# A four-block graph network on one core: the first unit's weights load later, mixing groups end with a block, four PSUM places for the first unit's tiles, batch norm by column chunk, the last bias goes into the residual

## The reference

```python
edge_index = jnp.stack([src, dst])
x = _layernorm(x + _L0_gnn_ref(x, ...))   # h = segment_sum(norm * (x @ W.T)[row]) + b; batch norm over nodes; exact gelu; + x
x = _layernorm(x + _L1_gnn_ref(x, ...))   # two layers relu(h @ W_self + mean_of_neighbours(h) @ W_neigh + b)
x = _layernorm(x + _L2_gnn_ref(x, ...))   # two gated relational layers: w = einsum('rb,bio->rio', att, basis), 30 bases, 2 relations, + x @ root + bias
x = _layernorm(x + _L3_gnn_ref(x, ...))   # x = h + segment_sum(h[send]); relu(x @ W1 + b1) @ W2 + b2
```

## Time and profile before

| what | value |
|---|---|
| median of 3 runs | 958.25 us (957.13 to 961.15) |
| profiled execution, its own time | 959.76 us |
| its span | 957.8 us |
| TensorE busy | 899.9 us, 94% |
| DVE busy | 684.1 us, 71% |
| ACT busy | 280.2 us, 29% |
| POOL busy | 85.5 us, 9% |
| mean granted TensorE clock | 0.977 |

### The profile page before, as it was taken

How to read it: one execution, slowest core, us unless ns; L and a number is a source line. 1 busy time by engine, 2 the same in 40 slices (tenths; PEclk the granted TensorE clock), 3 DMA queues, 4 the chain that set the end, 5 groups by cost and what they waited for, 6 DMA issues and landing times.

```text
span 957.8 us, 13083 instructions
## 1 busy us (share of the span) xinstructions
PE 899.9 (94%) x4320; PEld 434.2 (45%) x4320; DVE 684.1 (71%) x1469; ACT 280.2 (29%) x431; POOL 85.5 (9%) x66
## 2 busy tenths in 40 slices
PE   6799999998996999988799799999999999999996
PEld 2354555554554544433344344444444444444442
DVE  6598898854437879798899999999834244442358
ACT  0132345443873313424031211111711131132220
POOL 1000011120111002103021000000600010010000
PEclk9899999999997999999799999999999999999998
DMA  8755565558112495788644675664041014322236
GB/s 285 233 176 155 156 179 163 158 142 186 44 45 67 109 241 167 193 249 160 178 125 128 136 186 157 181 159 116 1 99 34 1 49 115 90 66 44 44 88 195
DMA packets 133371, 126.97 MB, mean 133 GB/s; under 512 B 80417, under 2 KB 80886, under 8 KB 133306
## 3 DMA queue, kind: packets, MB, share of 16 engines
q10 hardware_dynamic: 94784, 57.69, 24.5%
q1 hardware_dynamic: 38522, 68.45, 24.3%
HBM read 95.24 MB, written 12.52 MB: 113 GB/s over the span
## 4 chain that ended last, share of the span: by engine, by line
PE 65%; DVE 19%; DMA 6%; issue 3%; ACT 3%; DVEq 1%; POOL 1%; ACTq 1%; SPq 1%
PE Dp L669 23%; PE Dp L639 22%; PE T L595 9%; PE Dp L551 5%; PE Dp L694 5%; DVE acc L1205 4%; DMA stage<-in_basis 2%; DVE stt L1297 2%; DVE Zraw L1316 1%; DMA wst<-mixd 1%; DVE w L1334 1%; DVE Zraw L1274 1%; DVE S L1282 1%; POOL Zraw L508 1%; DMA Zraw<-in_basis 1%
## 5 line engine op out<-in xcount | busy, mean ns | idle before, releaser
L639 PE MATMUL Dp<-W,hT 128*128 128x512 f16 x816 | 182.9, 383 | 6.6 <-DMA hT<-S 3.2
L669 PE MATMUL Dp<-Zraw,A 128*128 128x512 f16 x800 | 173.0, 379 | 0.0
L1205 DVE SCALAR_TENSOR_TENSOR acc<-stage,att,acc 128x512 f32<-128x512 f32 x232 | 166.6, 788 | 4.0 <-DMA stage<-in_basis 4.0
L669 PE MATMUL Dp<-Zraw,AT 128*128 128x512 f16 x600 | 130.0, 379 | 0.0
L639 PEld LDWEIGHTS Dp<-W,hT 128*128 128x128 f16 x816 | 80.1, 99 | 103.6 <-issue 8.4
L669 PEld LDWEIGHTS Dp<-Zraw,A 128*128 128x128 f16 x800 | 78.3, 98 | 94.4
L1098 DVE TENSOR_SCALAR Zraw<-hT,w 128x640 f16<-128x640 f16 (+1 forms) x240 | 111.1, 463 | 0.1
L669 PEld LDWEIGHTS Dp<-Zraw,AT 128*128 128x128 f16 x600 | 58.7, 98 | 70.8
L1096 DVE TENSOR_SCALAR Zraw<-hT,w 128x128 f16<-128x128 f16 (+1 forms) x240 | 66.7, 278 | 27.0 <-PE Dp L551 18.1
L551 PE MATMUL Dp<-Zraw 128*128 128x320 f16 (+1 forms) x480 | 74.7, 302 | 1.6 <-DVE Zraw L1098 1.0
L922 ACT ACTIVATE Zraw<-Dp,zsc 128x512 f16<-128x512 f32 x50 | 32.2, 684 | 133.7 <-PE Dp L639 131.1
(11 more groups left out here) (169 smaller groups left out, 905.2 us busy)
## 6 DMA issues: line engine op xcount, KB each, us to landing
stage<-in_basis SPq DMA_DIRECT2D x180, 256.0 KB, 2.9
Zraw<-in_basis SPq DMA_DIRECT2D x60, 256.0 KB, 2.9
xres<-w ACTq DMA_DIRECT2D x30, 256.0 KB, 2.3
xr<-xres ACTq DMA_DIRECT2D x30, 256.0 KB, 2.9
wst<-in_Wn ACTq DMA_DIRECT2D x4, 1024.0 KB, 5.7
wst<-in_Ws ACTq DMA_DIRECT2D x4, 1024.0 KB, 5.6
wst<-mixd ACTq DMA_DIRECT2D x4, 1024.0 KB, 5.9
wst<-in_root ACTq DMA_DIRECT2D x3, 1024.0 KB, 5.7
```

Source lines behind the costliest of these rows:

```text
L639: last = nc.tensor.matmul(Dp[:, j, m, :], turned[:, hp, k * P:(k + 1) * P], weights_of(u, m)[:, wp, k, :], start=(n == 0), stop=(n == 3 * ...
L669: last = nc.tensor.matmul(sum_bank(t), a[:, k, ds(t * P, P)], Z[:, r, h, k, :], start=(n == 0), stop=(n == count - 1))
L1205: last = v.scalar_tensor_tensor(part, stage[:, q, :], a, part, ALU.mult, ALU.add)
```

## The change

Six edits:

1. ACT's first step is now the copy-out of mixing group 0; the load of W0 comes behind it. DVE takes W0's maximum behind the maxima of x, before window 10, and no longer before window 4.
2. `GROUP_BLOCKS` gives the seven later mixing groups 6, 6, 6, 6, 5, 5 and 6 windows, so that each group's last product is the last one behind a window.
3. Unit 0's dense tiles go to four PSUM places in turn, two in `Dp` and two in `T`, and tile t waits for DVE's read of tile t-4.
4. `agg_turned` has the column chunk as its outer loop: 20 matmuls fill one bank, then a signal; `block_stats` multiplies that chunk and takes its statistics. There are three parts instead of five, of 512, 512 and 226 columns.
5. Unit 4 adds unit 6's bias to its normalized rows (`w2 = w1 + bias`, a new DVE operation for each tile) and stores that sum to `xres`; the store waits for it (`s_rb`). The bias is loaded behind unit 4's last dense tile, earlier than before.
6. `last_tile` then needs one operation for what were two: `w2 = product * scale + xr`. TensorE's wait for a free PSUM place in unit 6 is now on that operation (`s_v`).

```diff
 MIX_SLOTS = 8
-PARTS = 5
+PARTS = 3
 KEYS = WIN * REL * NT
...
 
+        GROUP_BLOCKS = [6, 6, 6, 6, 5, 5, 6]
+        assert sum(GROUP_BLOCKS) == NWIN and len(GROUP_BLOCKS) == GROUPS - 1
+        SHARES = [(i + 1) * PAIRS // n - i * PAIRS // n for n in GROUP_BLOCKS for i in range(n)]
+
         def mix_share(w):
 
-            rest = PAIRS * (GROUPS - 1)
-            return (w + 1) * rest // NWIN - w * rest // NWIN
+            return SHARES[w]
 
         def groups_done(w):
 
-            rest = PAIRS * (GROUPS - 1)
-            return 1 + (w + 1) * rest // NWIN // PAIRS
+            return 1 + sum(SHARES[:w + 1]) // PAIRS
 
...
             ("agg", 4, 0): [("high", 5, 0)],
-            ("agg", 4, 1): [("bias", 6)],
+            ("dense", 4, 9): [("bias", 6)],
             ("agg", 4, 2): [("load", 6, 0)],
...
 
+        def dense_bank(u, t, m):
+
+            if u == 0:
+                return (Dp[:, 0, 0, :], Dp[:, 1, 0, :], T[:, 0, :], T[:, 1, :])[t % 4]
+            return Dp[:, t % 2, m, :]
+
+        def dense_rows(u, t, m):
+
+            return dense_bank(u, t, m).rearrange("p (a d) -> p a d", a=1)
+
         BACK = {(0, 0): 4, (0, 1): 5, (1, 0): 6, (2, 0): 7, (2, 1): 8, (3, 0): 9}
...
                 low_weights(1, m)
-            pool.wait_ge(s_agg[0], KT)
+            pool.wait_ge(s_agg[0], PARTS * KT)
             pool.wait_ge(s_dout, NT)
...
                     if nz:
-                        wait(pe, s_zlo[u], t - 1)
+                        wait(pe, s_zlo[u], t - 3 if u == 0 else t - 1)
                     if nz == 2:
                         wait(pe, s_zlp[u], t - 1)
-                    if unit["own"] is not None:
+                    if u == NU - 1:
+                        wait(pe, s_v, NT * LN.index(u) + t - 1)
+                    elif unit["own"] is not None:
                         wait(pe, s_own[u], t - 1)
...
                             for k in range(KT):
-                                last = nc.tensor.matmul(Dp[:, j, m, :], turned[:, hp, k * P:(k + 1) * P],
+                                last = nc.tensor.matmul(dense_bank(u, t, m), turned[:, hp, k * P:(k + 1) * P],
                                                         weights_of(u, m)[:, wp, k, :], start=(n == 0), stop=(n == 3 * KT - 1))
...
                     j = b % 2
-                    wait(pe, b_ev, b - 1)
-                    for k in range(NT):
-                        if b == 0:
-                            pe.wait_ge(s_zlo[0], k + 1)
-                        for h in range(2):
-                            for c in range(0, NP, D):
-                                w = min(D, NP - c)
+                    for i in range(PARTS):
+                        c, w = i * D, min(D, NP - i * D)
+                        wait(pe, b_ev, PARTS * (b - 2) + i + 1)
+                        for k in range(NT):
+                            if b == 0 and i == 0:
+                                pe.wait_ge(s_zlo[0], k + 1)
+                            for h in range(2):
                                 last = nc.tensor.matmul(Df[:, j, c:c + w], Z[:, 0, h, k, b * P:(b + 1) * P],
                                                         AT[:, k, c:c + w], start=(k == 0 and h == 0), stop=(k == NT - 1 and h == 1))
-                    last.then_inc(s_agg[0], 1)
+                        last.then_inc(s_agg[0], 1)
 
...
                 if u == 1:
-                    pe.wait_ge(b_ev, KT)
+                    pe.wait_ge(b_ev, PARTS * KT)
                     for t in range(4):
...
 
+            mixed_out(0)
             load_weights(0, 0)
-            mixed_out(0)
             for t in range(NT):
...
                     nc.scalar.activation(S16[:, ds(t, 1), 0:D], w1[:, j:j + 1, :], ACT.Copy, scale=LN_SCALE).then_inc(s_hi[u], 1)
-                    act.dma_start(xres[ds(t * P, P), :], w1[:, j, :]).then_inc(s_xst[u][j], 16)
+                    if u == 4:
+                        act.wait_ge(s_rb, t + 1)
+                    act.dma_start(xres[ds(t * P, P), :], (w2 if u == 4 else w1)[:, j, :]).then_inc(s_xst[u][j], 16)
 
...
                             scale = 2.0 ** -unit["zexp"]
-                        nc.scalar.activation(Z[:, r, 0, ds(t, 1), :], Dp[:, j, r:r + 1, :], ACT.Copy,
+                        nc.scalar.activation(Z[:, r, 0, ds(t, 1), :], dense_rows(u, t, r), ACT.Copy,
                                              scale=scale).then_inc(s_zhi[u], 1)
...
                 link(v.memset(i_in[:, u:u + 1], 1.0 / LN_SCALE))
-            weight_work("counts", 0, 0)
             windows_to(6)
...
             v.tensor_reduce(xin[:, :], xcol[:, :], AX.X, ALU.max).then_inc(s_xin, 1)
+            weight_work("counts", 0, 0)
             windows_to(13)
...
                     dve.wait_ge(s_zhi[u], t * nz + 1)
-                    v.scalar_tensor_tensor(Z[:, 0, 1, ds(t, 1), :], Dp[:, j, 0:1, :], scale,
+                    v.scalar_tensor_tensor(Z[:, 0, 1, ds(t, 1), :], dense_rows(u, t, 0), scale,
                                            Z[:, 0, 0, ds(t, 1), :], ALU.mult, ALU.subtract).then_inc(s_zlo[u], 1)
...
                         normalize(t, j)
+                        if u == 4:
+                            dve.wait_ge(s_bias[6], 16)
+                            dve.wait_ge(s_r, NT * u + t + 1)
+                            v.tensor_tensor(w2[:, j, :], w1[:, j, :], bias_of(6), ALU.add).then_inc(s_rb, 1)
                     else:
...
                     dve.wait_ge(s_d, t + (NT * u + 1))
-                    v.scalar_tensor_tensor(acc[:, 0, j, :], Dp[:, j, 0, :], ownc[:, u:u + 1], bias_of(u),
-                                           ALU.mult, ALU.add).then_inc(s_own[u], 1)
-                    dve.wait_ge(s_own[u], t + 1)
                     tile_moved(dve, s_xl[u], t, j)
                     if isinstance(t, int) and t < 2:
                         dve.wait_ge(s_ready, NT * u + NT - 1 + t)
-                    v.tensor_tensor(w2[:, j, :], acc[:, 0, j, :], xr[:, j, :], ALU.add).then_inc(s_v, 1)
+                    else:
+                        dve.wait_ge(s_r, NT * u + t - 1)
+                    v.scalar_tensor_tensor(w2[:, j, :], Dp[:, j, 0, :], ownc[:, u:u + 1], xr[:, j, :],
+                                           ALU.mult, ALU.add).then_inc(s_v, 1)
                     stats(t, j)
...
 
-                    dve.wait_ge(s_agg[0], b + 1)
-                    v.tensor_tensor(HT[:, b, :], Df[:, b % 2, 0:NP], drow, ALU.mult).then_inc(b_ev, 1)
-                    dve.wait_ge(b_ev, b + 1)
                     for i in range(PARTS):
-                        v.bn_stats(bst[:, b % 2, i * 6:(i + 1) * 6],
-                                   HT[:, b, i * (N // PARTS):(i + 1) * (N // PARTS)]).then_inc(b_st, 1)
+                        c, n = i * D, PARTS * b + i + 1
+                        dve.wait_ge(s_agg[0], n)
+                        v.tensor_tensor(HT[:, b, c:min(c + D, NP)], Df[:, b % 2, c:min(c + D, NP)], drow[:, c:min(c + D, NP)],
+                                        ALU.mult).then_inc(b_ev, 1)
+                        dve.wait_ge(b_ev, n)
+                        v.bn_stats(bst[:, b % 2, i * 6:(i + 1) * 6], HT[:, b, c:min(c + D, N)]).then_inc(b_st, 1)
                     dve.wait_ge(b_st, PARTS * (b + 1))
                     v.bn_aggr(bmv[:, b, :], bst[:, b % 2, :]).then_inc(b_mv, 1)
                     dve.wait_ge(b_mv, b + 1)
```

More of the change, by code:

```diff
@@ L248, in resnorm_gnn_kernel @@
         s_zlp = {u: sem(f"s_zlp{u}") for u in (3, 4)}
-        s_own = {u: sem(f"s_own{u}") for u in (1, 2, 3, 4, 6)}
+        s_own = {u: sem(f"s_own{u}") for u in (1, 2, 3, 4)}
         s_agg = {u: sem(f"s_agg{u}") for u in range(6)}
@@ L259, in resnorm_gnn_kernel @@
         s_gl = sem("s_gl")
+        s_rb = sem("s_rb")
         s_diag = sem("s_diag")
```

## The result

The changed kernel takes 950.65 us, the median of 5 runs (946.62 to 953.21); the kernel before takes 959.58 beside it (957.13 to 961.15, 5 runs). The ratio is 0.9903, with an interval of [0.9882, 0.9924]: 1.0% faster. The profiled execution took 948.84 us, span 946.9 (before 959.76, span 957.8), at a mean granted clock of 0.981 (before 0.977). By the medians the gain is 8.9 us, by the two profiles 10.9.

The account below looks back on a forecast made before the run. The ending chain was two thirds TensorE, a fifth DVE, so only TensorE's idle time or DVE tails could pay. Terms 0 - 2.1 - 3.2 - 2.5 + 0.4 - 3.8 = -11.2 us: profiled 948.6, median 947.0, range 943 to 952.5.

Parts of the forecast that it names:

- W0's load, 0: Start: TensorE begins about 1.5 us sooner, but late W0 may delay group 1's piece; 0, bounds -1.5 and +1.1.
- W0 out of the way: Rival: SP's early start is kept and nearly all of tile 2's wait goes; 944.5 us, chance 0.15.
- W0's maximum, 0: Before window 10: DVE's 2.29 us only changes order; 0, at worst part returns as a wait there.
- Window 10 takes the gain: Rival: DVE's 2.29 us shows whole, W0 collides (+1.1), transposes keep 1.7 of four places; 952.1 us, chance 0.14.
- Groups, -2.1: Windows: four TensorE waits go (-3.0 us), one product is paid later (0.9); bounds -3.0 and -1.0.
- Four places, -3.2: Unit 0's dense tiles: 4.6 us of tile 2's wait and slowness, less 0.5 and 0.9 for transposes; bounds -1.5, -4.6.
- Chunks, -2.5: Unit 0's tail: DVE's 3.2 us after the last matmul becomes 0.75; bounds -1.0 and -2.6 us.
- weight loads come into the open: Rival, slower: 98 ns of all 240 stationary loads exposed in column chunks, 23.5 us; 970.5 us, chance 0.02.
- Unit 4, +0.4: Before unit 5: the store of the sum waits for DVE's new operation, delaying z_out; bounds 0 and 1.0 us.
- unit 6, -3.8: Last unit: TensorE becomes the bound at 2.59 us a tile, 3.1 us plus 0.7 in the tail; bounds -2.0, -3.9.
- The late residual that was feared: Unit 6: the residual's load, 2.66 us with some 0.6 in hand, might be slower and lessen the gain.
- The early gains don't arrive: Rival: units 1 to 3 keep their own pace, 7.8 us of earlier gains lost, 3.4 stay; 954.9 us, chance 0.06.

Follow-up runs that it names:

- load_later: Changed kernel with unit 1's first weights (1 MB) and bias (256 KB) loaded behind unit 0's dense tile 2, not tile 0: 946.73 us, ratio 0.9868.
- two_places_later: Changed kernel with unit 0's dense tiles in two PSUM places, and unit 1's first weights and bias loaded behind dense tile 2: 950.21 us, ratio 0.9899.
- changed_again: The changed kernel itself, run and profiled once more for the scatter: 950.6 us, ratio 0.9902.
- chunks_apart: Changed kernel with unit 0's statistics taken by whole block in five pieces again, TensorE's loop as before: 950.67 us, ratio 0.9908.
- diag_later: Changed kernel with GpSimd's diagonal for unit 1 waiting for unit 0's batch norm coefficients: 947.67 us, ratio 0.9872.
- combo: load_later and diag_later together, plus the last store of unit 4's residual issued behind unit 5's first output: 945.1 us, ratio 0.9856.

## Why the prediction held, and where it did not

The time came out 3.7 us over the 947.0 and inside the range, and the profiled execution within 0.3 us of 948.6. That nearness is partly luck. The term for four places failed, and the start, window 10 and the early units gave 3.0 us that no edit is shown to have earned. The profiled execution also lies 1.8 us below its own median, and by the medians 8.9 us of the 11.2 arrived. The bounds of the terms, added by squares, give 944.7 to 950.3; the 943.5 to 951 of the prediction are wider, without a working.

**W0's load, 0.** Right in size, as far as the scatter lets one see; the ten late profiles average 0.3 us less than the two early ones, 30.4 against 30.7. Neither mechanism was right as it stood. By the row alone W0 would stay wholly behind SP's queue; it did so for four microseconds, and mixd's stores with it, and then shared. The Trainium skill ("DMA: Bandwidth & Descriptors", on arbitration) has each DMA engine go round between the queues it has work for: from 30 to 33 us, with 51.1% for q1 and 54.1% for q10, the trace agrees, and from 25 to 29 us, with 104.8% against 3.0%, it does not. The rival "W0 out of the way" fell: half of TensorE's earlier start of 1.2 us ends in a longer wait for the piece, 6.0 us on average against 5.4, and its landing scatters by 3 us.

**W0's maximum, 0.** Right, with a wrong tell-tale. Waits at window 10 of over 2 us were to disprove it; they came (2.30) and cost nothing: with window 1 equally slow the stretch takes 45.28 us with the early maximum and 1.14 us of waits, and 45.34 with the late one and 2.28. That fits DVE setting the pace there, as the prediction had it. "Window 10 takes the gain" fell too.

**Groups, -2.1.** Mechanism right, measured -2.8: the four waits went, and the product that was to be paid later cost 0.2 and not 0.9.

**Four places, -3.2.** This step failed: against before, +0.2 to +0.5 in the three profiles in which the clock fell, -1.5 in the four in which it held. Tile 2 behaved as forecast (0.54 for 0.5, and 0.51 to 1.08 over all with the edit). The term took tile 4's transpose to land after 6.5 us, as in the earlier trace rows; issued at the same distance from the first tile (7.02 against 6.93 us), it took 8.0, and 7.5 to 8.2 in all seven profiles with four places and the early load. So the wait is 2.45 in place of 0.9, and the slow tiles add 7.04 - 5.35 = 1.7: together 3.2, the whole of the term. (The 4.6 us it started from are 4.4: the slow tile's 4.24 is a duration and the 2.59 a distance between starts, and from start to start tile 2 took 4.03.) I had written this bound ("another microsecond or two on late transposes, or a lower clock after the pauses") and should have counted both at once. The load's part in the landing is shown by load_later, and two_places_later shows that the places and the load are two waits in series: from 35.11 moving the load alone takes off 0.55, the places alone 0.1 to 2.2, both 4.4. The 1.5 us by which the landing outgrew come with the places. Behind the early load tile 4's transpose lands after 6.5 and 6.4 us with two places and after 7.5 to 8.2 with four; ahead of the late one it is 3.2 with two and 4.7 and 5.0 with four. So the row's landing time did not hold for the kernel with four places. By what way the places make the transpose slower stays open.

**Chunks, -2.5.** The tail of the statistics shrank as worked out (0.75 forecast, 0.9 with the gaps). In the profile after 2.0 us arrived, but 0.3 of them are the two faster matmuls behind the gelu; like with like, changed_again against before and chunks_apart, it is 58.36 - 56.67 = 1.7. The missing part is ACT's wait of 0.73 us through GpSimd's operation, and diag_later and combo get it back (55.93 and 55.94, so 2.4 in all). The block's own 1.50 and 1.71 us used to cover it: chunks_apart and before have the small operation at 0.16 us. A cover that the edit itself took away was not in my sum. The rival that weight loads come into the open fell: the 240 matmuls take 43.28 us in every profile.

**Unit 4, +0.4; unit 6, -3.8.** Measured +0.53; and -3.8 in the profile after, -2.9 to -3.8 over all with the edit. The late residual that was feared shows as waits of 0.72 and 0.54 us on DVE; TensorE runs all ten tiles there without a gap.

**Early gains.** "The early gains don't arrive" fell: units 1 to 3 took 297.67 against 298.39. But that stretch scatters by 3.5 us between profiles. TensorE's busy time for the same matmuls goes from 279.7 to 282.7 us in it and its idle time from 15.9 to 17.8, so both have a part; the cause was not tested.

## What to carry to other kernels

When a wait is taken away, write out what the engine meets next with its landing time and with the clock after the pause, and look at what stands ahead of that transfer in its own queue: here moving a 1 MB load and a bias by two tiles was worth 2.2 to 3.9 us, up to as much again as the largest edit. Two waits in series hide each other, so try both edits together before either is judged. A gain of 2 us in 950 is read from a column of the trace that repeats within tenths, not from medians that scatter by 3, and columns are compared where the clock was the same.

## What the runs showed of the hardware

GpSimd held DVE back all at once and not by degrees. Beside GpSimd's 2.36 us operation DVE's product of a PSUM chunk, its statistics and their join ran at 0.42, 0.40 and 0.23 us; the first DVE operation that reads two tensors from SBUF stood until GpSimd was done (284.72 + 1.26 = 285.98 against 285.97), and the second again (286.02 + 0.35 = 286.37 against 285.93 + 0.43 = 286.36). The Trainium skill ("SBUF — State Buffer", on who interferes with whom) says that a DVE instruction with two SBUF inputs contends with a GpSimd instruction that reads SBUF, and that the later one is blocked whole; the trace agrees to 0.01 us.

With a 1 MB load and a 256 KB one ahead of them on the same queue, the transposes of tiles 4 and 5 landed after 6.2 to 8.2 us (nine profiles), and after 3.1 to 5.0 us without (three). With either order tile 4's took longer in the kernels with four places, by 1.0 us or more.

After TensorE's pause of 2.0 to 2.5 us the next 24 matmuls took 5.35 or 5.36 us in four profiles and 7.04 in three; the longest pause of the seven (2.52) is among those that kept the clock. Behind the wait for the piece, 4.9 to 8.2 us, window 1 took anything from 1.79 to 3.07 us.
